# Two rounds' evictions with preparation, routing and FFN steps between them; FFN by seven tiles; row halves

## The reference

```python
xn = _layernorm(x)
x = x + _L0_attn_ref(xn, ...) + _L0_ffn_ref(xn, ...)
xn = _layernorm(x)
x = x + _L1_attn_ref(xn, ...) + _L1_ffn_ref(xn, ...)
```

## Time and profile before

| | |
|---|---|
| median of 3 runs | 1660.05 us (1656.97 to 1660.71) |
| profiled execution, its own time | 1656.48 us |
| its span | 1654.8 us |
| granted PE clock, mean | 0.914 of full |
| instructions | 21187 |
| busy share PE / DVE / ACT / POOL | 73% / 80% / 88% / 25% |
| moved by DMA | 99.18 MB, 60 GB/s |

### The profile page before, as it was taken

How to read it: one execution, slowest core, us unless ns; L and a number is a source line. 1 busy time by engine, 2 the same in 40 slices (tenths; PEclk the granted TensorE clock), 3 DMA queues, 4 the chain that set the end, 5 groups by cost and what they waited for, 6 DMA issues and landing times.

```text
span 1654.8 us, 21187 instructions
## 1 busy us (share of the span) xinstructions
PE 1210.6 (73%) x7777; PEld 454.9 (27%) x7910; DVE 1327.9 (80%) x2465; ACT 1448.5 (88%) x716; POOL 411.6 (25%) x258
## 2 busy tenths in 40 slices
PE   4559565778798889888888888556766776776565
PEld 2123121214324423432432442332212222121112
DVE  6668565798798798788788789558988997998677
ACT  2487978789999999999999999909898988989996
POOL 2155360024622022022122212352212312220101
PEclk8589797889899899999999999889999999999898
DMA  5504325111231011111111112151033023121011
GB/s 135 158 16 141 97 50 164 38 29 53 66 129 36 26 39 33 26 38 39 26 42 30 26 42 56 39 127 48 19 105 75 25 100 70 29 75 49 20 29 51
DMA packets 100032, 99.18 MB, mean 60 GB/s; under 512 B 40402, under 2 KB 75346, under 8 KB 99922
## 3 DMA queue, kind: packets, MB, share of 16 engines
q1 hardware_dynamic: 95506, 86.72, 18.9%
q0 software_dynamic: 4416, 11.02, 2.6%
HBM read 52.75 MB, written 44.96 MB: 59 GB/s over the span
## 4 chain that ended last, share of the span: by engine, by line
ACT 54%; DVE 18%; PE 14%; issue 8%; POOL 2%; SPq 2%; DMA 2%; ACTq 0%; DVEq 0%; POOLq 0%
ACT scores L589 19%; ACT scores L578 18%; ACT exp L1075 13%; DVE exp L1081 7%; PE pvb L534 4%; PE ring L519 4%; DVE scores L553 4%; PE ring L1058 1%; ACT L589 1%; POOL x L389 1%; ACT ht L837 1%; PE ring L337 1%; PE aux L1021 1%; ACT L578 1%; DMA at<-att 1%
## 5 line engine op out<-in xcount | busy, mean ns | idle before, releaser
L553 DVE TENSOR_SCALAR scores<-ring 128x1024 f32<-128x1024 f32 x512 | 594.7, 1214 | 95.3 <-PE ring L519 94.9
L1075 ACT ACTIVATE exp<-ring 128x1024 f32<-128x1024 f32 x512 | 473.3, 1230 | 84.5 <-PE ring L1058 80.4
L578 ACT ACTIVATE scores<-scores 128x8192 f32<-128x8192 f32 x60 | 418.1, 7023 | 45.7 <-DVE scores L553 45.6
L589 ACT ACTIVATE scores<-scores 128x8192 f32<-128x8192 f32 x64 | 445.9, 7020 | 0.2
L1081 DVE SCALAR_TENSOR_TENSOR exp<-exp 128x512 f32<-128x512 f32 x512 | 380.0, 765 | 51.8 <-ACT exp L1075 51.2
L1058 PE MATMUL ring<-stk 128*128 128x512 bf16 x998 | 302.3, 394 | 143.7 <-ACT exp L1075 139.2
L534 PE MATMUL pvb<-scores,val 128*9 128x256 f32 x4096 | 328.5, 398 | 104.2 <-ACT scores L589 74.9
L519 PE MATMUL ring<-stk 128*128 128x512 bf16 x917 | 298.8, 401 | 47.6 <-issue 17.5
L1058 PEld LDWEIGHTS ring<-stk 128*128 128x128 bf16 x1024 | 68.5, 100 | 372.0 <-ACT exp L1075 301.3
L534 PEld LDWEIGHTS pvb<-scores,val 128*9 128x9 f32 x4096 | 66.3, 90 | 328.7 <-issue 324.6
L519 PEld LDWEIGHTS ring<-stk 128*128 128x128 bf16 x1024 | 63.7, 99 | 246.1 <-issue 156.1
(11 more groups left out here) (225 smaller groups left out, 1104.0 us busy)
## 6 DMA issues: line engine op xcount, KB each, us to landing
stk<-stack SPq DMA_DIRECT2D x128, 192.0 KB, 2.9
stack<-qp SPq DMA_DIRECT2D x8, 768.0 KB, 3.7
stack<-kp SPq DMA_DIRECT2D x8, 768.0 KB, 6.9
xj<-xg SPq DMA_DIRECT2D x12, 384.0 KB
yg<-yj POOLq DMA_DIRECT2D x12, 384.0 KB, 3.3
stack<-qp SPq DMA_DIRECT2D x8, 512.0 KB, 4.6
stack<-kp SPq DMA_DIRECT2D x8, 512.0 KB, 5.5
xg<-attg SPq DMA_DIRECT2D x5, 512.0 KB, 5.0
```

The source lines that it names most:

```text
L553: nc.vector.tensor_scalar(S[place][:, j * N:(j + 1) * N], tile, 1e-12, None, ALU.max).then_inc(o.release(("qk", group, place, j)), 1)
L578: nc.scalar.activation(S[place][:], S[place][:], ACT.Sqrt).then_inc(root_done, 1)
L589: nc.scalar.activation(S[place][:], S[place][:], ACT.Exp, scale=-1.0).then_inc(exp_done, 1)
L1075: nc.scalar.activation(EX[i // 2][:, i % 2, :], tile, ACT.Exp, scale=SCALE1).then_inc(o.release(("qk1", n, i)), 1)
```

## The change

- **Between the rounds.** The preparation of batch r+1 (without the row sums), the routing (end of round 3) and the placing (end of round 4) leave the 32 steps and stand behind the last eviction of their round, before or behind the FFN steps. The row sums go to step 8 of the next round. The router's inputs are loaded at place 2 of round 3 instead of place 1.
- **FFN by seven tiles**, in ten rounds (3 to 12) instead of twelve by six; the last part ends after round 13. Layer 2's (the code's layer 1's) batch 0 is prepared after rounds 13, 14 and 15.
- **Row halves.** Each layer 0 stack is loaded twice, into partitions 0 to 53 and 64 to 117; each of the two score products of a step uses one copy (64 rows) instead of both using one stack in 128 rows.
- **Start.** x comes in two halves; the first deviation is ACT's root and DVE's reciprocal; the angle reduction, `stk0` memsets and some loads move to POOL, some loads to ACT's queue; only the first four heads' stacks are stored before round 0, the other twelve and v behind the first two stack loads.
- **Layer 1.** The first three score tiles are issued ahead of the last place's value product. Of the 128 tiles of batches 0 to 2, 23 get their sum from ACT's accumulator and no fold on DVE (`sum_by_act`). PE's preparation steps are cut into pieces of two to four matmuls at successive tiles, and DVE reads them three or four tiles later.

```diff
+SIDES = [slice(0, 64), slice(64, 128)]
-JOBS = 6
+JOBS = 7
-FIRST_JOBS, LAST_JOBS = 3, 14
+FIRST_JOBS, LAST_JOBS = 3, 12
+def sum_by_act(n, i):
+    s = n % H * NT + i
+    return n < HEADS - H and 12 <= s < 104 and s % 4 == 1
...
         def load_stack0(sp, n, slot, done):
-            sp.dma_start(stk0[slot][0:SUM_ROW], d["stack0"][n * HD:(n + 1) * HD].rearrange("e r s t -> (e r) s t")
-                         ).then_inc(done, 16)
-            sp.dma_start(stk0[slot][SUM_ROW:ROWS], d["sums0"][n]).then_inc(done, 16)
+            for side in SIDES:
+                sp.dma_start(stk0[slot][side.start:side.start + SUM_ROW],
+                             d["stack0"][n * HD:(n + 1) * HD].rearrange("e r s t -> (e r) s t")).then_inc(done, 16)
+                sp.dma_start(stk0[slot][side.start + SUM_ROW:side.start + ROWS], d["sums0"][n]).then_inc(done, 16)
...
-            for cols in HALVES:
-                mm = nc.tensor.matmul(tile[:, cols], stk0[slot][:, K, j * P:(j + 1) * P], stk0[slot][:, Q, cols],
+            for side, cols in zip(SIDES, HALVES):
+                mm = nc.tensor.matmul(tile[:, cols], stk0[slot][side, K, j * P:(j + 1) * P], stk0[slot][side, Q, cols],
                                       start=True, stop=True)
...
+            if sum_by_act(n, i):
+                if n >= 2 * GROUP:
+                    act.wait_ge(w_done, n // GROUP - 1)
+                nc.scalar.activation(EX[i // 2][:, i % 2, :], tile, ACT.Exp, scale=SCALE1,
+                                     accum_out=den[n // GROUP % 2][:, n % GROUP, i:i + 1]
+                                     ).then_inc(o.release(("qk1", n, i)), 1)
...
-        ATURN_AT, AWO_AT, ADD_AT, STATS1_AT, NORMAL_AT, TURN1_AT = 2, 6, 10, 27, 40, 49
-        Q1_AT, K1_AT, SPLIT1_AT, V1_AT, MIX_AT, FTURN_AT, FWO_AT = 55, 59, 64, 72, (78, 88), 96, 102
+        FTURN_AT, FWO_AT, ATURN_AT, AWO_AT = 4, 10, 18, 24
+        ADD_AT, STATS1_AT, NORMAL_AT, TURN1_AT = 34, 50, 60, 69
+        Q1_AT, K1_AT, SPLIT1_AT, V1_AT, MIX_AT = 75, 80, (84, 86, 88, 90), 92, (99, 106)
...
             def fast(pe):
...
+                    if r < B - 1:
+                        pe_turn0(pe, o, r + 1)
+                        for name in "qk":
+                            pe_project0(pe, o, r + 1, name)
+                        pe_value0(pe, o, r + 1)
+                        pe_route0(pe, o, r + 1)
...
+                    if r == CHOOSE_ROUND:
+                        pe_rank(pe, o)
+                    if r == ATT1_ROUND:
+                        at_once(pe_turn_att(pe, o, 0, None))
+                        at_once(pe_project_att(pe, o, 0, None))
+                    if r == TURN1_ROUND:
+                        pe_prepare1(pe, o, 0)
                 for place in range(GROUP):
+                    if place == GROUP - 1:
+                        for i in range(RING):
+                            pe_scores1(pe, o, 0, i)
...
             def fast(sp):
                 sp.wait_ge(ones_stored, 32)
+                sp.wait_ge(first_stored, 128)
                 stack(0)
                 stack(1)
-                for place in range(GROUP):
-                    load_values(sp, place, place)
-                clear_places(sp)
+                store_prepared(sp, o, 0)
+                store_prepared_sums(sp, 0)
...
+                        if place == 2 and 1 <= r < B:
+                            store_prepared_sums(sp, r)
                             if r == FIRST_JOBS:
                                 wait_prepared(sp, B - 1)
...
                                 load_router(sp)
                                 load_shared_weights(sp)
                                 load_jobs(sp, o, r)
                                 load_own_tokens(sp)
...
             def fast(dve):
...
+                    if r < B - 1:
+                        project0(o, r + 1)
+                        if r + 2 < B:
+                            for t in range(NT):
+                                dve_stats0(dve, chain, r + 2, t)
+                            dve_variance(dve, chain, var_ready)
+                        else:
+                            dve_clip(dve, o)
...
+                    if r == CHOOSE_ROUND:
+                        at_once(dve_choose(dve, chain))
+                        dve_keep_ranks(dve, o)
+                    if r == PLACE_ROUND:
+                        at_once(dve_place(dve, o, chain))
+                    if r == ATT1_ROUND:
+                        dve_keep_att(dve, o, 0)
+                        dve_add_att(dve, o, 0)
+                    if r == ADD1_ROUND:
+                        begin1(o, chain, 0)
+                    if r == TURN1_ROUND:
+                        turn1(o, chain, 0)
```

More of the change, by code:

```diff
@@ L477, in act_first @@
+            act.wait_ge(k_ready, 1)
+            nc.scalar.activation(sk[:], kf0[:], ACT.Square).then_inc(sk_ready, 1)
+            act.wait_ge(qr_ready, 1)
+            nc.scalar.activation(qp0[:, 1, :], qf0[:], ACT.Copy).then_inc(q_half, 1)
             tile = o.filled(act, ("sums0", 0))
[L478 to L479 removed]
+            nc.scalar.activation(sump[:, 0, :], tile[0:64, :], ACT.Copy)
@@ L487, in dve_first @@
+            pool.wait_ge(q_half, 1)
+            nc.gpsimd.tensor_tensor(qp0[:, 2, :], qf0[:], qp0[:, 1, :], ALU.subtract).then_inc(q_split, 1)
         def dve_first(dve, o, chain):
-            dve_keep_v0(dve, o, 0)
-            dve_keep_route0(dve, o, 0)
-            dve.wait_ge(qk_f, 1)
-            chain.step(nc.vector.tensor_tensor(qf0[:], qf0[:], qp0[:, 0, :], ALU.subtract))
+            tile = o.filled(dve, ("k0", 0))
+            nc.vector.tensor_scalar(kf0[:], tile, early["bk0"], None, ALU.add).then_inc(k_ready, 1)
@@ L1286, in _ @@
             mm.then_inc(ring_full, 1)
+            pe_value0(pe, o, 0)
+            pe_route0(pe, o, 0)
             tile = o.begin(pe, ("count", 0))
             pe.wait_ge(held, 2)
-            nc.tensor.matmul(tile[0:1, 0:4], ones_col[:], within[:], start=True, stop=True).then_inc(ring_full, 1)
+            nc.tensor.matmul(tile[0:1, 0:4], ones_col, within[:], start=True, stop=True).then_inc(ring_full, 1)
             def general(pe):
@@ L1403, in fast @@
[L1403 to L1410 removed]
+                                value = pe_value1(pe, o, b + 1, AUX)
@@ new lines, in fast @@
+                            if V1_AT <= s < V1_AT + 4:
+                                next(value)
+                            for i, start in enumerate(MIX_AT):
+                                if s == start:
+                                    mix = pe_mix(pe, o, b + 1, i, AUX)
+                                if start <= s < start + 4:
+                                    next(mix)
+                at_once(pe_turn_end(pe, o, B - 1, AUX))
+                at_once(pe_project_end(pe, o, B - 1, None))
@@ L1593, in _ @@
         def _(pool):
-            chain = Chain(pool, pool_steps)
-            nc.gpsimd.memset(power[:], -0.5).then_inc(pool_steps, 1)
-            chain.count = 1
-            nc.gpsimd.memset(ones_rows[:], 1.0).then_inc(ones_made, 1)
-            chain.wait()
-            pool_deviation(pool, 0, var_ready, std_ready)
+            rows = early["rows"]
+            pool.dma_start(rows[:], d["early_rows"].to_broadcast([P, rows.shape[1]])).then_inc(rows_in, 16)
+            rows = fixed["rows"]
+            pool.dma_start(rows[:], d["fixed_rows"].to_broadcast([P, rows.shape[1]])).then_inc(rows_in, 16)
+            nc.gpsimd.memset(power, -0.5).then_inc(pool_steps, 1)
+            nc.gpsimd.memset(ones_rows[:], 1.0).then_inc(ones_made, 1)
+            for i in range(2):
+                nc.gpsimd.memset(stk0[i][:].rearrange("r s t -> r (s t)").bitcast(F32), 0.0).then_inc(zeroed, 1)
+            pool.wait_ge(pool_steps, 1)
+            pool.wait_ge(xn_ready, NT)
+            reduce_angles(pool)
             pool_first(pool)
+            pool.wait_ge(trig_done, 1)
+            pool.dma_start(d["cs"], cs0[:]).then_inc(cs_stored, 16)
             def general(pool):
@@ L1801, in fast @@
                 o, chain = fast_order, Chain(dve, dve_steps, done)
-                choosing, placing = dve_choose(dve, chain), dve_place(dve, o, chain)
                 for r in range(GROUPS):
```

612 lines of the change are left out of this document (313 added, 299 removed).

## The result

The changed kernel takes 1574.20 us, the median of 4 runs (1573.78 to 1575.30), where the kernel before took 1658.51 in runs beside it (4 runs, 1654.55 to 1660.71). The ratio is 0.950, with a 95% interval from 0.948 to 0.951. The profiled execution took 1573.78 with a span of 1572.1, and that is to be held against the 1548.8 to which the terms were summed, from 1656.48 of the profiled execution before. So the change gave 82.7 us of the 107.7 that I had added up. 25 us are missing.

A forecast was written before the change was run, and what follows sets the result against it. ACT was taken as the bound, busy 1448.5 of 1654.8 us. The terms sum to -107.7, from 1656.5 to 1548.8; half of the median's 3.5 us excess added gives 1551, likeliest 1536 to 1567, range 1529 to 1584.

The forecast's parts named there:

- Start and round 0: Layer 0's start: first eviction at 43.5 us, last root of round 0 at 82.1 instead of 104.65, -22.5 us.
- Waits of rounds 1 to 4: Layer 0: ACT's waits at the roots vanish because the 32 steps hold nothing but one sums eviction, -45.7 us.
- Behind round 3: Layer 0: new ACT wait from late tokens, up products, choosing and ranks after the last eviction, +3 us (0 to 5).
- Behind round 4: Layer 0: new ACT wait from FFN then placing, 9 us undisturbed, 19 with DVE meeting POOL's two multiplies; taken as +15.
- Steady loop: Layer 0's steady rounds: evictions 38.5 plus FFN 21.6 make 60.1 us, nothing over against ACT; +3 us (0 to 16).
- Row halves: Layer 0 score products: no gain or loss on the path, as DVE sets the pace of the steps, 0 us.
- FFN in ten rounds: Layer 0: tanh 10 times 2.15 us in place of 12 times 1.9, -1 us.
- Passage: Between the layers: ACT's idle time falls from 41.5 to 3 us, -38.5 us.
- ACT's accumulator: Layer 1: 69 sums on ACT cost 0.19 us each, +13 us (5.5 to 26).
- Waits in layer 1: Layer 1: DVE's relief and PE's cut pieces reduce ACT's waits from 43.0 to 9 us, -34 us (-40 to 0).
- layer 1 keeps its waits: Rival, 11%: DVE keeps colliding with POOL or the ring of three PSUM tiles starves at each piece; 1585 us.

The follow-up runs named there:

- e4: The changed kernel with POOL's two multiplies of the first FFN round waiting until DVE has placed the tokens: 1563.81 us.
- e7: The changed kernel with row halves undone (one stack of 128 rows, one load, both products over all rows): 1572.20 us.
- e6: The changed kernel without sums on ACT, all 512 folds on DVE: 1586.74 us.
- e8: The changed kernel with each auxiliary tile of layer 1 issued whole where its first piece stood, DVE's readings unmoved: 1578.79 us.
- e2: The changed kernel with auxiliary tiles counted on their own semaphore and DVE's readings of them 3 tiles earlier in its order: 1523.30 us.
- e1: The changed kernel with layer 1's auxiliary PSUM tile counting its fillings on its own semaphore instead of the one shared with score tiles: 1561.91 us.
- e9: e2 without sums on ACT, run on another chip: 1583.04 us, ratio 0.935 to the kernel before.
- e11: The changed kernel with own counter, early readings, POOL's multiplies after placing, and row halves undone, on another chip: 1551.45 us, ratio 0.916.

## Why the prediction was right and wrong

In the order of its sum, each with what was measured:

- **Start and round 0**: -22.5 forecast, -20.1 measured. The first eviction came at 46.30 instead of 43.5.
- **Waits of rounds 1 to 4**: -45.7, all gone as forecast.
- **Behind round 3**: +3 forecast, 0. **Behind round 4**: +15 forecast, +16.5, and by the mechanism named. Its parts: 9 undisturbed and up to 10 for the collision were forecast; by e4 they are 6.8 and 9.7.
- **Steady loop**: +3 forecast, 0. The DVE loop of a round took less than I had it at. These are the last take-out of a round, the first eviction of the next and its last take-out:

```profile
507.74 0.41 DVE L592 COPY ot<-pvb 128x256 f32<-128x256 f32 x1
...
528.02 9.13 DVE L587 TENSOR_SCALAR scores<-ring 128x1024 f32<-128x1024 f32 x8
...
566.63 0.41 DVE L592 COPY ot<-pvb 128x256 f32<-128x256 f32 x1
```

  From the last take-out to the next round's first eviction pass 20.3 us (20.3 to 21.0 behind rounds 5 to 8, while DVE catches up), where I had 21.6, and the 32 evictions take 38.6, where I had 38.5. Together 58.9, under ACT's 60.36. The seventh tile costs about its sixth, as I had it, but I counted from the longest stretch: from the first transpose to the last up product PE took 15.1 to 16.8 us before (16.8 in round 8, from which I read, 16.3 in the middle one of eleven), and takes 18.3 to 19.0 now. 16.3 x 7/6 is 19.0.
- **Row halves**: 0 forecast. e7 confirms it, and PE shows no sign of a mode change that costs: a pair of 64-row products takes 0.41 us where one of 128 rows takes 0.62, so the two overlap. Where PE waits for nobody, its step from one value product to the next is 0.87 us in the changed kernel and 1.09 in e7, shorter by one whole product:

```profile
587.49 0.62 PE L568 MATMUL pvb<-scores,val 128*9 128x256 f32 x8
...
588.36 0.62 PE L568 MATMUL pvb<-scores,val 128*9 128x256 f32 x8
```

```profile
600.82 0.62 PE L568 MATMUL pvb<-scores,val 128*9 128x256 f32 x8
...
601.91 0.62 PE L568 MATMUL pvb<-scores,val 128*9 128x256 f32 x8
```

- **FFN in ten rounds**: -1 forecast, 10 x 2.24 us of tanh after 12 x 1.95, so -1.0.
- **Passage**: -38.5 forecast, -39.4 (2.12 left of 41.5).
- **ACT's accumulator**: +13 forecast. Its record is never under 0.19 us, but the next exp starts 0.09 behind it, 69 x 0.09 = +6.2:

```profile
1040.28 0.31 ACT L1134 ACTIVATION_READ_ACCUMULATOR exp<-ring 128x1 f32 x1
1040.37 2.96 ACT L1138 ACTIVATE exp<-ring 128x1024 f32<-128x1024 f32 x3
```

- **Waits in layer 1**: -34 forecast (43.0 to 9). Measured 48.7 less the 2.12 of the passage, 46.6: +3.6. **This is the step that failed**, by 38 us; the rest together was 13 us too dear, which leaves the 25. (The measured terms add up to 79.9 of the 82.7. Of the missing 3 us, 2 lie in layer 1: net of the passage it grew by 530.6 - 522.8 = 7.8, and the last two terms say 9.8. I can't place them.)

The words of that step were that DVE's relief and PE's pieces would take the waits, and that "k's projection comes two tiles behind the eviction of q, which I count at under 1 us each batch". Relief and pieces work as it said: e6 and e8 put them at 12.6 and 8.2 us here (for the pieces 4.6 by the medians). What I left out of the sum is what the pieces brought with them. To read a tile whose last piece comes 2 or 3 score tiles behind its first, DVE's readings were moved back by 3 and 4 places, while the next auxiliary tile mostly stands only 5 to 7 places behind, 2 or 3 behind the reading (`k1` and `v1` are 12 apart, and there is no wait). With a ring of three PE can run up to three tiles ahead of ACT, so none is left. I priced that for k alone and took a stop of PE for its length only, without the ring that runs empty behind it at PE's lower clock. And the open place in the count, which can be read from `begin` and `then_inc`, I didn't see. e2 shows these new costs to be 532.7 - 483.8 = 48.9 us, 12.0 of them by the counter alone (e1) and 36.9 more by the early readings on top of it: as much as the whole of the old waits and a little more, so that nothing of the gain was to be seen. How much of the 36.9 is the length of PE's stops and how much its lower clock behind them was not taken apart. How much of the 43.0 of before had each cause isn't known; no experiment was made on the kernel before.

The rival "layer 1 keeps its waits" named 1585 and had 11%. Its outcome came true, and the measured time is 11 us below it. Of its two mechanisms the starved ring was there; that DVE collides with POOL wasn't what mattered.

The measured 1574.20 lies in the range of 1529 to 1584, but above the 1536 to 1567 that I held likeliest, and that it lies in the range at all is in part luck: the waits of layer 1 were missed by 38 us, and the other terms, 13 us too dear, took a third of that back. With those other terms as forecast it would have been 1587.

## What to carry to other kernels

When work is cut into pieces and spread over a pipeline, ask of each semaphore that counts in order whether an open piece holds up what comes behind it; give such a tile its own counter. In a queue that runs in order, measure the distance from the reading of a buffer to its next filling in the producer's time, not in the consumer's: subtract how far the producer runs ahead. And two gains that are real (pieces and relief) can be hidden to the last microsecond by new waits, so a stage that doesn't move is worth taking apart before it is called bound.

## What the runs showed of the hardware

- A VectorE instruction of seven columns lasted 5.27 us when it met a GpSimd multiply of 2464 columns, and six of one column 5.14 more than with the multiply out of the way (e4); both ended with the multiply. In these two meetings VectorE was held until the other was through, and its own size, one column or seven, made no difference. The Trainium skill, *GPSIMD Engine Reference*, Specifications, names VectorE's instructions with two SBUF inputs and its two-port modes as those that contend. The seven-column one has one tensor input; the trace doesn't show its mode.
- On the chip of e9 to e11, PE, DVE and ACT nearly stand still during most of the time in which GpSimd issues the 32 indirect DMAs that place tokens (353.75 to 394.0 in e11). The kernel before took 33 us more there too (1692.69 to 1659.87); no trace of it on that chip was kept, so that its loss is the same one is not shown. In e11:

```profile
367.99 7.03 ACT L620 ACTIVATE scores<-scores 128x8192 f32<-128x8192 f32 x1 [7.45 <-issue]
...
378.03 1.23 DVE L595 TENSOR_SCALAR scores<-ring 128x1024 f32<-128x1024 f32 x1 [9.75 <-remote]
...
390.62 0.58 PE L576 MATMUL pvb<-scores,val 128*9 128x256 f32 x1 [2.21 <-issue]
...
398.34 5.75 DVE L595 TENSOR_SCALAR scores<-ring 128x1024 f32<-128x1024 f32 x5 [19.08 <-remote]
```

  From 380.8 to 397.6 PE's records are single matmuls, 2.1 to 2.8 us from start to start, with nothing in the profile that they wait for, and DVE and ACT do nothing; the evictions run again from 398.34, 4 us behind the last indirect DMA. On the other chips the same stretch shows no such thing. What differs there stays open.
